# A transformer block with x and context laid out turned, normalized by GpSimd with rows that go through memory

## The reference

```python
shift_a, scale_a, gate_a, shift_m, scale_m, gate_m = split(silu(c) @ W_mod + b_mod, 6)
x_norm = _ln(x) * (1 + scale_a) + shift_a
q, k, v = split(x_norm @ W_qkv + b_qkv, 3)
x = x + gate_a * (attention(q, k, v) @ W_proj + b_proj)
q_c = _ln(x) @ W_qc + b_qc
k_c, v_c = split(_ln(context) @ W_kvc + b_kvc, 2)
x = x + attention(q_c, k_c, v_c) @ W_cproj + b_cproj
x_norm2 = _ln(x) * (1 + scale_m) + shift_m
x = x + gate_m * (gelu(x_norm2 @ W_mlp1 + b_mlp1) @ W_mlp2 + b_mlp2)
```

## Time and profile before

| | us |
|---|---|
| median of 3 runs | 901.58 |
| lowest, highest | 899.60, 903.73 |
| profiled execution, its time | 899.01 |
| profiled execution, its span | 897.2 |
| granted TensorE clock, mean | 0.973 |

### The profile page before, as it was taken

The page is one execution under the profiler, slowest core; times in us unless marked ns, Lnnn a source line. Parts: engine busy times, 40 slices in busy tenths (PEclk is TensorE's granted clock), DMA queues, the critical chain, the costliest instruction groups (busy, mean ns, idle before and its releaser), DMA issues.

```text
span 897.2 us, 19234 instructions
## 1 busy us (share of the span) xinstructions
PE 836.8 (93%) x7088; PEld 636.3 (71%) x7088; DVE 640.4 (71%) x1370; ACT 495.8 (55%) x934; POOL 354.4 (40%) x400
## 2 busy tenths in 40 slices
...
DMA packets 79784, 79.27 MB, mean 88 GB/s; under 512 B 12681, under 2 KB 74250, under 8 KB 79306
## 3 DMA queue, kind: packets, MB, share of 16 engines
...
## 4 chain that ended last, share of the span: by engine, by line
PE 76%; DVE 13%; issue 4%; ACT 2%; POOL 2%; SPq 1%; DMA 1%; DVEq 0%; POOLq 0%; ACTq 0%
PE bank L673 19%; PE scan L762 13%; PE bank L706 12%; PE pv L719 12%; PE bank L697 7%; PE score L772 5%; PE bank L686 4%; PE bank L652 4%; DVE MX_x L1048 3%; DVE xn_y L938 2%; DVE MX_y L1048 1%; DVE stats_y L927 1%; DVE PN L971 1%; SPq L426 1%; DVE x L996 1%
## 5 line engine op out<-in xcount | busy, mean ns | idle before, releaser
L891 ACT ACTIVATE P<-score 128x512 f32<-128x512 f32 x512 | 286.0, 597 | 208.8 <-PE score L772 205.8
L1048 DVE TENSOR_REDUCE MX_x<-scan 128x2 fp32r<-128x512 f32 x256 | 166.6, 676 | 59.1 <-PE scan L762 58.8
L1048 DVE TENSOR_REDUCE MX_y<-scan 128x2 fp32r<-128x512 f32 x256 | 167.1, 679 | 41.4 <-PE scan L762 41.4
L673 PE MATMUL bank<-xT_y,W 128*128 128x256 f32 x960 | 134.9, 297 | 3.9 <-POOL xT_y L558 2.6
L673 PEld LDWEIGHTS bank<-xT_y,W 128*128 128x128 f32 x960 | 123.6, 198 | 11.8 <-issue 4.7
L706 PE MATMUL bank<-w_down,HH 128*128 128x256 f32 x512 | 127.6, 395 | 1.0 <-ACT HH L853 1.0
L762 PE MATMUL scan<-KS_x,QS_x 63*128 63x256 f32 x512 | 110.4, 327 | 10.3 <-DVE MX_x L1048 6.7
L772 PE MATMUL score<-QS_y,KS_y 64*128 64x256 f32 x512 | 107.3, 317 | 2.8 <-ACT P L891 2.7
L762 PE MATMUL scan<-KS_y,QS_y 63*128 63x256 f32 x512 | 103.0, 315 | 6.9 <-DVE MX_y L1048 5.5
L762 PEld LDWEIGHTS scan<-KS_y,QS_y 63*128 63x128 f32 x512 | 70.7, 187 | 53.9 <-issue 29.0
L706 PEld LDWEIGHTS bank<-w_down,HH 128*128 128x128 f32 x512 | 94.8, 194 | 19.1 <-ACT HH L853 1.7
(11 more groups left out here) (112 smaller groups left out, 1278.7 us busy)
## 6 DMA issues: line engine op xcount, KB each, us to landing
KS_x<-SK SPq DMA_DIRECT2D x96, 128.0 KB, 2.1
QS_x<-SQ_x SPq DMA_DIRECT2D x96, 128.0 KB, 2.1
KS_y<-SK SPq DMA_DIRECT2D x96, 128.0 KB, 2.6
QS_y<-SQ_y SPq DMA_DIRECT2D x96, 128.0 KB, 2.1
x_in<-in_x SPq DMA_DIRECT2D x16, 256.0 KB, 2.8
c_in<-in_ctx SPq DMA_DIRECT2D x16, 256.0 KB, 3.2
gate_a<-d_gate SPq DMA_DIRECT2D x16, 256.0 KB, 3.5
gate_m<-d_gate SPq DMA_DIRECT2D x16, 256.0 KB, 3.5
```

The lines of the kernel that those rows point to most:

```text
L673: last = nc.tensor.matmul(to[:, i * N:(i + 1) * N], w[p][:, c, (blk + i) * 128:(blk + i + 1) * 128], xT[k][:, q, c, :], start=(n == 0), st ...
L891: nc.scalar.activation(P[:, s % 8, :, :].rearrange("p a n -> p (a n)"), score_bank[s % 2][:, :], ACT.Exp, scale=SCALE).then_inc(s_exp, 1)
L1048: nc.vector.tensor_reduce(MX[s1][:, half, col:col + NB], scan_bank[n % NSCAN][:, :].rearrange("p (a n) -> p a n", a=NB), AXIS.X, ALU.max, ...
```

## The change

The host lays x and context out a second time with the channels on the partitions (xT, ctxT). SyncE loads them into tn_x and tn_c. The statistics are still taken by VectorE with tokens on the partitions. GpSimd's root now writes mean and 1 / sqrt side by side into ST; SyncE stores ST to a row of memory (d_st, 512 numbers) and loads that row into all 128 partitions of MR, which x and context share. GpSimd then subtracts and multiplies tn by rows of MR, read with a step of four numbers (`norm_turned`). TensorE's transposes T_x and T_c go. ACT's modulation T_x reads tn_x; T_c is a cast and a subtraction on GpSimd, and ACT's copy and VectorE's subtraction for it go. x_in and c_in come free once the statistics are taken. NPV is 1 and NBANK 3. Two small tiles of the start (silu, bv) now lie in OT. All tables are new.

In the repeated sections x's way is: st_x (SyncE, A slot 9), mr_x (B, 2), norm_x of the next round's list as GpSimd's first entry, T_x (ACT, A slot 3), T_x (GpSimd). The diff, cut; of the tables one line of TensorE's stands:

```diff
-NSCAN, NPV, NBANK = 2, 2, 2
+NSCAN, NPV, NBANK = 2, 1, 3
 FIRST, LAST = -1, B + 2
+ROWS_X = 1
...
-    "A": [("pv_x3", -1, 1), ("v_xa", 0, 1), ("v_xb", 0, 2), ("up0a", -3, 3), ("up0b", -3, 3), ("up1a", -3, 3),
+    "A": [("pv_x3", -1, 1), ("v_xa", 0, 1), ("v_xb", 0, 1), ("up0a", -3, 1), ("up1a", -3, 3), ("up2a", -3, 3),
...
-BANKED = {"up0", "up1", "up2", "up3", "out_x", "out_y", "T_c", "T_y", "T_x",
+BANKED = {"up0", "up1", "up2", "up3", "out_x", "out_y", "T_y",
           "T_m", "k_x", "q_x", "k_y", "q_y", "v_x", "v_y", "down0", "down1"}
-HALVED = BANKED - {"T_c", "T_y", "T_x", "T_m"}
+HALVED = BANKED - {"T_y", "T_m"}
...
-        xn = {k: sb(f"xn_{k}", [128, NB, H]) for k in "xy"}
-        xn["c"], xn["m"] = xn["x"], xn["y"]
+        xn = {"y": sb("xn_y", [128, NB, H])}
+        xn["m"] = xn["y"]
+        tn = {k: sb(f"tn_{k}", [128, CB, N]) for k in "xc"}
+        ST = {k: sb(f"ST_{k}", [128, 2, NB]) for k in "xc"}
+        MR = sb("MR", [128, 128 * 2 * NB])
...
+        d_st = {k: dram(f"d_st_{k}", (2, 128 * 2 * NB)) for k in "xc"}
...
+            sp.dma_start(tn["x"][:, :, :], xT_in[0]).then_inc(s_tn["x"], 16)
...
+            sp.dma_start(tn["c"][:, :, :], ctxT_in[0]).then_inc(s_tn["c"], 16)
...
-                    sp.wait_ge(s_xn["x"], b - 1)
+                    sp.wait_ge(s_stats["x"], b - 1)
                 sp.dma_start(x_in[b % 2][:, :, :], x[b].rearrange("(a p) c -> p a c", p=128)).then_inc(s_x[b % 2], 16)
 
             def load_c(b):
                 if b == 0:
                     return
-                sp.wait_ge(s_xn["c"], b)
+                sp.wait_ge(s_stats["c"], b)
                 sp.dma_start(c_in[:, :, :], ctx_in[b].rearrange("(a p) c -> p a c", p=128)).then_inc(s_c, 16)
+
+            def load_turned(k, b):
+                if b == 0:
+                    return
+                if k == "x":
+                    sp.wait_ge(s_xm["x"], b)
+                else:
+                    sp.wait_ge(s_xT["c"], b)
+                sp.dma_start(tn[k][:, :, :], {"x": xT_in, "c": ctxT_in}[k][b]).then_inc(s_tn[k], 16)
+
+            def store_rows(k, b):
+                sp.wait_ge(s_mean[k], b + 1)
+                sp.wait_ge(s_rstd[k], b + 1)
+                sp.dma_start(d_st[k][b % 2:b % 2 + 1, :].rearrange("o (p k) -> (o p) k", p=128),
+                             ST[k][:, :, :].rearrange("p k a -> p (k a)")).then_inc(s_st[k], 16)
+
+            def load_rows(k, b):
+
+                sp.wait_ge(s_st[k], 16 * (b + 1))
+                if k == "x":
+                    wait(sp, s_xn["c"], b - ROWS_X)
+                else:
+                    sp.wait_ge(s_xn["x"], min(b + ROWS_X + 1, B))
+                wait(sp, s_xn[k], b)
+                sp.dma_start(MR[:, :], d_st[k][b % 2:b % 2 + 1, :].to_broadcast([128, 128 * 2 * NB]))\
+                    .then_inc(s_mr[k], 16)
...
+                    store_rows("x", 0)
+                    load_rows("x", 0)
...
+                to = ST[k][:, 1, :] if k in "xc" else rstd[k][:, :]
+                if k in "xc":
+                    wait(pool, s_st[k], 16 * b)
+                    nc.gpsimd.tensor_copy(ST[k][:, 0, :], mv[k][:, :, 0]).then_inc(s_mean[k], 1)
                 nc.gpsimd.tensor_tensor(var_eps[k][:, :], mv[k][:, :, 1], eps[:, :], ALU.add).then_inc(s_ve[k], 1)
                 pool.wait_ge(s_ve[k], b + 1)
-                nc.gpsimd.tensor_tensor(rstd[k][:, :], var_eps[k][:, :], minus_half[:, :],
-                                        ALU.pow).then_inc(s_rstd[k], 1)
-
-            def norm(k, src, b):
-                root(k, b)
-                pool.wait_ge(s_rstd[k], b + 1)
-
+                nc.gpsimd.tensor_tensor(to, var_eps[k][:, :], minus_half[:, :], ALU.pow).then_inc(s_rstd[k], 1)
+
+            def norm_m(b):
+                root("m", b)
+                pool.wait_ge(s_rstd["m"], b + 1)
+                pool.wait_ge(s_hi["T_y"], min(b + 2, B))
+                for a in range(NB):
+                    last = nc.gpsimd.tensor_scalar(xn["m"][:, a, :], x2[:, a, :], mv["m"][:, a, 0:1],
+                                                   rstd["m"][:, a:a + 1], ALU.subtract, ALU.mult)
+                last.then_inc(s_xn["m"], 1)
+
+            def norm_turned(k, b):
+                pool.wait_ge(s_mr[k], 16 * (b + 1))
+                pool.wait_ge(s_tn[k], 16 * (b + 1))
+                rows = MR[:, :].rearrange("q (p k a) -> q k a p", k=2, a=NB)
+                t = tn[k][:, :, :].rearrange("q c (a p) -> q c a p", a=NB)
+                nc.gpsimd.tensor_tensor(t, t, rows[:, 0:1, :, :].to_broadcast([128, CB, NB, 128]),
+                                        ALU.subtract).then_inc(s_centred[k], 1)
+                pool.wait_ge(s_centred[k], b + 1)
+                nc.gpsimd.tensor_tensor(t, t, rows[:, 1:2, :, :].to_broadcast([128, CB, NB, 128]),
+                                        ALU.mult).then_inc(s_xn[k], 1)
+
+            def split(k, b):
+
+                src = tn["c"] if k == "c" else xm
                 if k == "x":
-                    wait(pool, s_hi["T_c"], b - 1)
+                    pool.wait_ge(s_xm["x"], b + 1)
+                    wait(pool, s_V["x"], b)
                 if k == "c":
-                    pool.wait_ge(s_xm["x"], min(b + 2, B))
+                    pool.wait_ge(s_xn["c"], b + 1)
+                    wait(pool, s_V["y"], b)
                 if k == "m":
-                    pool.wait_ge(s_hi["T_y"], min(b + 2, B))
-                for a in range(NB):
-                    last = nc.gpsimd.tensor_scalar(xn[k][:, a, :], src[:, a, :], mv[k][:, a, 0:1], rstd[k][:, a:a + 1],
-                                                   ALU.subtract, ALU.mult)
-                last.then_inc(s_xn[k], 1)
-
-            def split(k, b):
-                pool.wait_ge(s_xm[k], b + 1)
-
-                if k == "x":
-                    wait(pool, s_V["x"], b)
-                else:
+                    pool.wait_ge(s_xm["m"], b + 1)
                     pool.wait_ge(s_lo["q_y"], min(b + 2, B))
-                nc.gpsimd.tensor_copy(xT[k][:, HI, :, :], xm[:, :, :]).then_inc(s_xT_hi[k], 1)
+                nc.gpsimd.tensor_copy(xT[k][:, HI, :, :], src[:, :, :]).then_inc(s_xT_hi[k], 1)
                 pool.wait_ge(s_xT_hi[k], b + 1)
-                nc.gpsimd.tensor_tensor(xT[k][:, LO, :, :], xm[:, :, :], xT[k][:, HI, :, :].bitcast(fp32),
+                nc.gpsimd.tensor_tensor(xT[k][:, LO, :, :], src[:, :, :], xT[k][:, HI, :, :].bitcast(fp32),
                                         ALU.subtract).then_inc(s_xT[k], 1)
...
-                "norm_x": lambda b: norm("x", x_in[b % 2], b),
-                "root_y": lambda b: root("y", b),
-                "norm_c": lambda b: norm("c", c_in, b),
-                "norm_m": lambda b: norm("m", x2, b),
-                "T_x": lambda b: split("x", b),
-                "T_m": lambda b: split("m", b),
+                **{f"root_{k}": lambda b, k=k: root(k, b) for k in "xyc"},
+                **{f"norm_{k}": lambda b, k=k: norm_turned(k, b) for k in "xc"},
+                "norm_m": norm_m,
+                **{f"T_{k}": lambda b, k=k: split(k, b) for k in "xcm"},
                 "gate": gate, "x_bias": biased_x, "x1_bias": biased_x1, "x2_bias": biased_x2,
                 "sum0": lambda b: total(0, b), "sum1": lambda b: total(1, b),
             }
 
+            root("x", 0)
...
-                **{f"T_{k}": lambda b, k=k: transposes(f"T_{k}", k, b) for k in "xycm"},
+                **{f"T_{k}": lambda b, k=k: transposes(f"T_{k}", k, b) for k in "ym"},
...
-            def modulated(name, k, col, b):
+            def modulated(k, col, b):
                 if k == "x":
                     wait(act, s_xT["m"], b - 3)
+                    act.wait_ge(s_xn["x"], b + 1)
+                    src = tn["x"]
                 else:
                     act.wait_ge(s_xT["x"], min(b + 4, B))
-                src = full(act, name, b)
+                    src = full(act, "T_m", b)[:, :].rearrange("p (c n) -> p c n", c=CB)
                 for c in range(CB):
-                    last = nc.scalar.activation(xm[:, c, :], src[:, c * N:(c + 1) * N], ACT.Identity,
+                    last = nc.scalar.activation(xm[:, c, :], src[:, c, :], ACT.Identity,
...
-                wait(dve, s_xn[k], b)
+                if k in "xc":
+                    wait(dve, s_mean[k], b)
+                    wait(dve, s_ve[k], b)
+                else:
+                    wait(dve, s_xn[k], b)
...
-                "T_c": lambda b: split_copied("T_c", "c", b),
...
+    def turned(name):
+        return np.asarray(inputs[name]).reshape(B, N, CB, 128).transpose(0, 3, 2, 1)
...
+        "xT": turned("x"),
+        "ctxT": turned("ctx_1024"),
```

More of the change, by code:

```diff
@@ L85 @@
+    "BB+1": [],
+    "BB+2": [("down1b", -3, 7)],
+    "B-1": [("k_xa", 1, 13), ("k_xb", 1, 13), ("q_xa", 1, 13), ("q_xb", 1, 13)],
 }
 ACT_PLAN = {
-    "A": [("v_x", 0, 2), ("up0", -3, 3), ("up1", -3, 3), ("up2", -3, 3), ("up3", -3, 3), ("T_x", 1, 3), ("k_x", 1,
```

(28 more changed lines are left out.)

210 lines of the change are left out of this document (98 added, 112 removed), and 35 rows, old and new, of tables (DVE_PLAN, PE_PLAN).

## The result

The changed kernel takes 925.21 us (median of 4 runs, 916.76 to 926.47), the kernel before in the same series 902.13 (4 runs, 899.60 to 903.73). The ratio is 1.0238, with a 95% interval of 1.0173 to 1.0304: slower, by 2.4%, where 889 us had been forecast, and outside the range of 874 to 910.

A forecast was written before the change was run, and what follows sets the result against it. TensorE, busy 93% of the span, was taken as the bound. 899.0 - 12.3 (transposes) - 11 (waits) + 11.5 (start) = 887.2 us, 889.8 in the median's terms, put down as 889; range 874 to 910.

The forecast's parts named there:

- GpSimd inside the period: Section A, before out_x: rows, norms and gate end at 9.3 us, needed at 10.4; 1.1 us slack, cost 0.
- Rival 1: GpSimd's norms: strided read dearer by a half, 1.92 us an instruction, out_x late; 899 us, no change; chance 0.15.
- rival 2: norm_x, gate, out_x (L600, L625, L755): the rows become the bound, chain 2.6 us later; 919 us, slower; chance 0.17.
- The transposes: TensorE: eight of 16 transposes per batch go, 28 groups at 0.44 us, saving 12.3 us.
- The waits: TensorE's waits, T_y for norm_y and x's scan for VectorE's maxima: 7 and 4 us saved, 11 in all.
- Banks: One bank for values, covered by three slots or more; third shared bank relaxes hardly any waits: 0.
- SyncE's load: SyncE and transfers: six more per batch, 3 us of issues in a queue with room, 1 MB more: 0.
- The start: Before the first projection: x's rows stored and loaded behind queued transfers, no cover; everything 11.5 us late.

The follow-up runs named there:

- the rows between: Changed kernel with SyncE's load of x's rows moved behind k_y's stacks and ahead of the output store: 897.94 us, ratio 0.9962.
- the rows early: Changed kernel with SyncE's load of x's rows issued right after the turned inputs, ahead of k_y's stacks and the output store: 882.09 us, ratio 0.9799.
- the transposes back: Both plus four unused identity transposes ahead of k_x's and of k_y's first real matmul: 889.14 us.
- Both: Changed kernel with the rows' load right after the turned inputs and gate ahead of norm_x: 876.57 us, 878.85 when run again.
- the third edit of the start: Both with x0's rows before later weight loads, T_x before root_x, and now x2's turned load and row store before q_x's stacks, row load before k_x's: 876.11 us.

## Why the prediction was wrong

**The step that failed** is the last one of GpSimd inside the period: "About 1.1 us of slack: I take 0". It was 2.3 us of lateness. Counted in us from the start of section A, in the period shown (the stall there is 2.44 us, the mean of the 12 is 2.2):

| | forecast | measured |
|---|---|---|
| rows' load issued | 1.8 | 3.3 |
| its landing | 3.5 | 4.6 |
| two norms | 2.7 | 3.1 |
| gate | 1.3 | 1.3 |
| gated weights there | 9.3 | 12.2 |
| needed | 10.4 | 9.9 |

- *The issue.* I began with y at the end of down1, as in the trace before. In the new order PN (1.19 us) and the low part of k_y (0.86) stand ahead of y on VectorE, so y comes 1.25 us later. That alone would have put the issue at about 3.1. And I had left out that k_y's stacks stand ahead of the output and the rows on SyncE, though I had listed them: an issue of 0.5 us was priced, the wait in front of it was not. In the period shown the two came together, sum1 at 315.07 and the last stack at 315.13, and either would have held the output; the rows between showed that k_y alone holds the load until 2.7 us.
- *The landing.* 3.5 us was that of gate_a, which has no transfer just ahead of it. Here the output's 256 KB stand there: 1.1 us more in this period, 0.6 by the medians, taken away by the same experiment.
- *The norms.* 1.28 us was the price of reads without a step; with the step it is 1.55. Rival 1 had this mechanism, at 0.64 us an instruction, more than twice what was measured; it alone turns nothing.
- *The need.* The section itself had become 0.5 us shorter, by TensorE's gains: what one engine gains, the covers of the others lose.
- *The clock.* I priced a us of stall as a us. It was 1.6 in these periods (26.6 us of idle, 16.8 of slower matmuls) and 1.2 in those of the rows between.

This is rival 2, with its place (L600, L625, L755) and near its time (919 us), to which I gave 0.17. "Each part of it has a row" was no ground against it: the rows were from places with nothing queued in front.

**The transposes.** 12.3 us forecast, 10.3 measured: right, somewhat high.

**The waits.** 11 us forecast, about double measured: the 12 periods of the rows early are 31.9 us shorter than before, and 8.1 of that are the transposes. T_y's wait is gone whole in them. TensorE's idle time falls from 16.4 to 2.0 us; and its busy time, compared at as many instructions (the transposes back), from 585.8 to 577.5, most of it in the scans and scores of section B (151.5 us before, 143.1 now), which follow one another more closely. Whether the third shared bank or the tables bring that isn't separated; a kernel with the new tables and the old banks wasn't tried.

**Banks and SyncE's load.** 0 forecast. No wait for pt appears, and 117 GB/s in the fast versions against 90 hold nothing up; right, but the order in SyncE's queue was no 0.

**The start.** 11.5 us forecast, first scan 12.1 us later: right at this place, and its cause too (the queue ahead of the store). Two slips in that sum are small: it adds 5.3 us where the sentence ahead has 5.5, and 17.0 + 3.5 is 20.5. But the steady part begins 19.8 us later. Between the first scan and there 7.7 us more are lost. Two things are seen there: the rows of the third x wait behind 12 stacks (their norm starts at 77.2 us), and the clock is at 0.72 from 30 to 120 us, where before it was 0.87 in the 90 us that correspond. Both's two runs differ by 8.4 us along with such a difference in the clock; that the late rows cost anything is not shown, as the third edit of the start moved them by 8 us and won nothing clear. The forecast had no term for either. The end gives 5.0 us back, which no term had and whose cause stays open.

Without the failed step the sum would have been near, 889 forecast and 882 for the rows early, but partly by luck: the waits gave 13 us more than forecast and the end 5, while the start took 8 more and the transposes gave 2 less.
